# Identity products in TensorE's waits: a two-layer graph and mixer kernel on one core

## The reference, cut to what matters

```python
xn = layernorm(x)                                     # x: 1024 x 512, fp32
x = x + dense_attention(xn, edges) + mixer0(xn)       # one head, 1024 x 1024 mask from edge counts
x = x + quantised_linear(layernorm(x))
xn = layernorm(x)
x = x + gnn(xn, edges) + linear_attention(xn)         # gnn: 2 layers, 8 heads, batch norms, MLP 512-256-512,
                                                      # a layer norm at its end
y = layernorm(x)
x = x + y + nibble_features(y)                        # 6 features a token -> three small MLPs -> 32 columns
```

## Time and profile before

| | |
|---|---|
| Runs, us | 1021.54, 1022.92, 1023.52 (median 1022.92) |
| The profiled execution, us | 1021.41, its span 1019.6 |
| TensorE busy | 951.3 us, 93% of the span |
| VectorE, ScalarE, GpSimd busy | 61%, 48%, 25% |
| Mean granted TensorE clock | 0.986 of 2.4 GHz |
| Chain that ended last | 75% TensorE, 7% GpSimd, 6% VectorE, 3% ScalarE |

### The profile page before, as it was taken

How to read it: one execution, slowest core, us unless ns; L and a number is a source line. 1 busy time by engine, 2 the same in 40 slices (tenths; PEclk the granted TensorE clock), 3 DMA queues, 4 the chain that set the end, 5 groups by cost and what they waited for, 6 DMA issues and landing times.

```text
span 1019.6 us, 15256 instructions
## 1 busy us (share of the span) xinstructions
PE 951.3 (93%) x5371; PEld 678.4 (67%) x5378; DVE 625.5 (61%) x1087; ACT 494.2 (48%) x767; POOL 251.1 (25%) x138
## 2 busy tenths in 40 slices
PE   5999999999998999999999999999999999999915
PEld 2745545788776886886777776746777777777313
DVE  4676466558777325428667776436576666746395
ACT  1655344554724223307666666223476666651054
POOL 2000000499943051310000029112100000570400
PEclk9999999999999999999999999999999999999968
DMA  9201100000200031145655574111065665632102
GB/s 328 76 0 42 42 1 22 1 1 1 83 1 1 3 121 42 58 149 160 190 168 165 176 244 140 42 42 42 14 195 180 187 184 171 226 85 68 38 1 82
DMA packets 58848, 96.14 MB, mean 94 GB/s; under 512 B 8284, under 2 KB 38172, under 8 KB 58270
## 3 DMA queue, kind: packets, MB, share of 16 engines
q1 hardware_dynamic: 55454, 93.11, 28.4%
q10 hardware_dynamic: 3328, 2.15, 0.7%
HBM read 59.58 MB, written 33.55 MB: 91 GB/s over the span
## 4 chain that ended last, share of the span: by engine, by line
PE 75%; POOL 7%; DVE 6%; issue 6%; ACT 3%; DMA 1%; SPq 0%; DVEq 0%; ACTq 0%; POOLq 0%
PE slots L1809 66%; PE slots L1876 9%; POOL MASK L710 3%; POOL MASK L704 1%; POOL KR L709 1%; DMA W<-in_wkT 1%; POOL X L741 1%; POOL PT L701 1%; ACT X L1126 1%; DVE X L1694 0%; POOL WL L721 0%; DVE SM L1671 0%; DVE st L1171 0%; ACT XTR L824 0%; DVE st L1657 0%
## 5 line engine op out<-in xcount | busy, mean ns | idle before, releaser
L1809 PE MATMUL slots<-PT,XN 128*64 128x256 f32 x1024 | 117.6, 382 | 0.2 <-DMA PT<-blocks 0.2
L1809 PE MATMUL slots<-KS,QS 64*128 64x512 f32 x768 | 107.3, 406 | 4.0 <-DVE nm L1599 2.9
L1599 DVE CUSTOM_DVE_ANT_0 SM<-slots,MASK 128x1024 f32<-128x1024 f32 x64 | 75.7, 1220 | 50.6 <-PE slots L1809 50.3
L1809 PEld LDWEIGHTS slots<-PT,XN 128*64 128x64 f32 x1024 | 72.0, 137 | 42.5 <-issue 11.4
L766 POOL TENSOR_TENSOR QS<-QF,QS 128x512 fp32r<-128x512 f32 x16 | 20.7, 1292 | 319.0 <-ACT QS L1046 319.0
L1809 PEld LDWEIGHTS slots<-KS,QS 64*128 64x128 f32 x768 | 72.5, 184 | 22.9 <-issue 9.4
L1030 ACT ACTIVATE SM<-SM,nm 128x1024 f32<-128x1024 f32 x64 | 73.4, 1146 | 24.2 <-DVE nm L1599 23.6
L813 ACT ACTIVATE PT<-slots 128x1024 f32<-128x1024 f32 x68 | 69.3, 1019 | 32.0 <-PE slots L1876 27.1
L1030 ACT ACTIVATE PT<-PT,nm 128x1024 f32<-128x1024 f32 x64 | 73.3, 1145 | 14.7 <-DVE nm L1599 14.0
L1809 PE MATMUL slots<-PT 128*128 128x512 bf16 (+3 forms) x401 | 77.6, 363 | 2.7 <-ACT PT L813 1.2
L1599 DVE CUSTOM_DVE_ANT_0 PT<-slots,MASK 128x1024 f32<-128x1024 f32 x64 | 75.2, 1211 | 4.1 <-PE slots L1809 3.9
(11 more groups left out here) (403 smaller groups left out, 2153.0 us busy)
## 6 DMA issues: line engine op xcount, KB each, us to landing
blocks<-FL SPq DMA_DIRECT2D x56, 512.0 KB, 3.2
PT<-blocks SPq DMA_DIRECT2D x224, 128.0 KB, 3.4
X<-in_x SPq DMA_DIRECT2D x4, 512.0 KB, 11.7
W<-in_wout SPq DMA_DIRECT2D x2, 1024.0 KB, 6.3
W<-in_gq SPq DMA_DIRECT2D x2, 1024.0 KB, 5.0
W<-in_gk SPq DMA_DIRECT2D x2, 1024.0 KB, 5.3
spill<-X SPq DMA_DIRECT2D x4, 512.0 KB, 2.6
SXR<-XTR SPq DMA_DIRECT2D x1, 2048.0 KB, 8.4
```

The lines of the kernel that those rows point to most:

```text
L1599: nc.vector.tensor_tensor_reduce(out=SMs[n % SMB], in0=src, in1=MASK[:, unit(n)[2], :], scale=-1.0, scalar=-0.1 * NO_EDGE, op0=ALU.add, op ...
L1809: return nc.tensor.matmul(o_, lhsT, rhs, start=start, stop=stop)
```

## The change

TensorE multiplies the identity (in one place the identity with the first chunk of XT) into parts of PSUM that a later job overwrites with its own first product: seven times ahead of the waits of "before", six times ahead of the waits for M's weights, twelve times between the turns of chunks 0 to 2 and those of chunk 3, and twice, and nine times with 512 columns, ahead of the wait for the features. Between the last two stands a new wait for six row sums.

```diff
+            def keep_busy(dst, rhs, count):
+
+                for _ in range(count):
+                    mm(dst, ident[:], rhs, True, True)
+
             def mixer_step(name, i):
 
                 slot = begin(name, i)
                 if name == "before":
+                    keep_busy(slot_of("M", 0)[:, 0:P], ident[:], 7)
                     pe.wait_ge(sums_made, 2)
                     pe.wait_ge(bnd_made, 1)
...
                 elif name == "M":
+                    if i == 0:
+                        keep_busy(slot[:, 0:P], ident[:], 6)
                     w_ready(pe, "wqT")
                     w_ready(pe, "wkT")
...
             for j in range(4):
                 begin("gT", j)
                 turn_chunks(j, range(FC - 1))
+            keep_busy(slot_of("gT", 0)[:, (FC - 1) * P:D], ident[:], 12)
             for j in range(4):
                 end(turn_chunks(j, [FC - 1]))
 
+            keep_busy(begin("fT", 0)[:, 0:P], ident[:], 2)
+            wait(y_summed, TT - 2)
+            keep_busy(slot_of("fT", 0)[:, 0:D], XT[:, 0, 0:D], 9)
             pe.wait_ge(hid_ready, 1)
             for q in range(2):
                 slot = begin("fT", q)
```

## The result

| | before | after |
|---|---|---|
| Median of 15 runs, us | 1023.48 (1020.96 to 1025.02) | 1025.91 (1023.45 to 1030.10) |
| Ratio, 95% interval | | 1.0026 [1.0013, 1.0038] |
| The profiled execution, us (its span) | 1021.41 (1019.6) | 1027.32 (1025.5) |
| TensorE busy | 951.3 us, 93% | 969.7 us, 95% |
| Mean granted clock in it, of 2.4 GHz | 0.986 | 0.986 |

The interval is +1.3 to +3.9 us. I had forecast 1023.9 and "within 0.2%" as the likeliest: the time lies in the range given (1022.0 to 1026.0), the change is a small but real loss, and its size, 2.7 us by the ratio, is over two and a half times the 1.0 us that I had forecast (1022.92 to 1023.9). The same kernel before had a median of 1022.92 in its first 3 runs and of 1023.48 in these 15. The page of after has 18 us more of TensorE at work; VectorE (626.0), ScalarE (494.2) and GpSimd (251.2) do the same as before.

What follows compares the result with a forecast made beforehand. TensorE was busy 93%, paced by its sequencer at the start; VectorE and ScalarE set the tail. Terms -0.1 + 0 + 1.6 + 0 + 0.1 = +1.6 on 1021.4 gave 1023.0, plus 0.9 of run excess 1023.9 us; range 1022.0 to 1026.0.

Steps and rivals of the forecast that it cites:

- the credit: Run median's 1.5 us excess over the profiled execution: a late tail clock rise avoided, so only 0.9 us stays.
- M is paced by the sequencer: Start: TensorE's sequencer reading bounds takes 1.98 us a group, so warm multiplications gain only 0.1 us.
- same price: VectorE's register loads cost about 0.5 us each, taken as showing the same price as TensorE's loads in M.
- Seven and six products at 0: Start blocks ahead of "before" and M: they fill waits or their overrun is caught up, cost 0.
- Two MATMULs a product: Twelve products before the last state chunk: 24 instructions, 2.6 us in a 1.0 us hole, cost +1.6 us.
- The rival that a product is one instruction: Block before the last state chunk: products take only 1.3 us, cost +0.3 us, the lower bound; no separate chance given.
- Two products at 0: Two products in fT's slot: four instructions, under 1 us, nothing behind them, cost 0.
- The wide block starts at half rate: Nine wide products before the features: 9.3 to 10.7 us, tail delay 1.6 to 2.4 us, adding 0.1 to the sum.
- rival (a): Slower: clock rises only after 6 us or more of the wide block, all 1.5 us excess stays; 1025.2 us, chance 0.26.
- (b): The runs' whole 1.5 us excess over the profiled execution goes: 1023.0 us or a little less, chance 0.20.
- (c): Faster: M's head start gets through (-0.9), the 1.5 us excess goes, 24 instructions fit their hole; 1020.5 us, chance 0.07.
- (d): Blocks do not act on the clock: wide block runs 15.4 us, 7 us late; 1030 us, chance 0.02.

Runs made afterwards that it cites:

- the repeat: The whole change unchanged, measured again in 12 runs against the kernel before: 1025.83 us against 1023.85, ratio 1.0017 [1.0001, 1.0032].
- all_blocks_spread: The whole change plus the four mixer outputs placed one to a gap, against the kernel before: 1027.37 us, ratio 1.0050.
- no_chunk_block_spread: The change without the twelve products before the last chunk, mixer outputs one to a gap, against the kernel before: 1024.65 us, ratio 1.0021.
- reads_moved_start_blocks: Kernel before with half of the bounds reads moved from M into kq, plus the seven and six start products: 1030.58 us, ratio 1.0074.
- reads_moved: Kernel before with half of the bounds reads moved from M into kq, no identity products: 1028.73 us, ratio 1.0055.
- only_start_blocks: Kernel before with only the seven and six products at the start: 1024.72 us, ratio 1.0002 [0.9987, 1.0017].
- no_chunk_block: The change without the twelve products before the last chunk, old job order, against the kernel before: 1025.51 us, ratio 1.0002.
- fitted_blocks: Kernel before with four products before the last chunk, two small and five wide ahead of the features, none at the start: 1024.22 us, ratio 1.0000.
- gaps_filled: Kernel before with mixer outputs one to a gap, nine products ahead of k1, eight ahead of each layer's gv: 1022.76 us, ratio 0.9990.

## Why the prediction was off: the mechanisms held, the credit did not

- **M is paced by the sequencer: right.** 2.00 us a group against 1.98 predicted; -0.1 predicted, +0.1 measured (17.19 against 17.07), which is no difference either way, and taking half of the reads away made the same warmth worth 2.8 us. The "same price" on VectorE is looser than the text has it: 0.5 us a load there against 1.98 / 3 = 0.66 here.
- **Seven and six products at 0: right.** They end at 8.64 and before 10.9; the wait for wkT still takes 0.98 us. The clock had risen within them (12 instructions in 1.60 us). That a wait is left was luck with wkT: in five of the six other profiles with start blocks M's first product stands right behind the block, yet M takes no longer than in the profiles without them (16.68 to 17.14 us in the four with all reads in place), as the sequencer's beat would have it.
- **Two MATMULs a product, 24 x 0.11 in a hole of 1.0 us, +1.6: right.** 2.68 us between the starts, VectorE 1.61 us later, the tail +1.61 with this block alone. The rival that a product is one instruction is out.
- **Two products at 0: right**, 1.22 us at half rate, nothing behind them.
- **The wide block starts at half rate, ends 9.3 to 10.7 us later, and ScalarE hides most of that: right, with the bound a little short.** 9.46 to 10.86 us in six profiles. By itself +0.14 us; with the chunk block +1.60 to +2.43, against bounds of 1.6 to 2.4 and a middle of 1.7. In three of the six profiles the clock rose late under the block (10.41 us and more), and the wide block's own share of the tail is 0.3 us in the mean of the six, where the sum has 0.1.
- **The Trainium skill's rule, that transposes don't count for the clock** ("TensorE: Matmul & The Clock Gate", Part 4): this case stays with its trace. By that rule the products of hid would begin at half rate in every run of before. In the profile of before they run at full rate behind 16 turns. It is the only one: in the eight other profiles without the features' block hid's first two instructions take 1.06 to 1.18 us instead of 0.70, so there the clock rose only after they had begun.
- **The step that failed is the last of the sum**: "I let a bit over half, 0.9 us, stay", which credits the change with 0.6 of the 1.5 us by which the median stood over the profiled execution, as lost by a late rise in the tail. The late rise exists and is the usual case, but it is cheap: in those eight profiles the 14 products behind it take 3.69 to 4.15 us, 0.16 us over the 3.71 of before in the mean and 0.44 at most. The features' block, which removes it, gained nothing that the runs can tell: 1.0001 [0.9990, 1.0012] alone (this interval by itself would still hold 0.6 us). What the profiled execution lacked lies mostly in the middle. It had about 29 us at half rate: 23.9 in the tail, one dip of 3.4 at 310, and 2 behind TensorE's last work; a mean run has 33 to 36. The middle follows its dips. In the order of jobs of before it is 945.15, 945.19 and 945.72 us in the three profiles with 3.4 us at half rate there, 946.62 with 6.8, and 948.37 to 948.92 in the four with 10.2. Over the runs of before in a set the time goes with the time at half rate (correlation 0.71 to 0.94, 0.26 to 0.36 us each): the 4 to 7 us that the mean run has more make 1.1 to 2.6 us, the size of the excess of 1.5. The dips are a few microseconds each: the one at 310 in all profiles but one, others at 93 to 99, 150, 330, 698 and 973, in other places in each execution.

Redone: without the credit the sum is +1.6 against the median, with 0.3 for the wide block and nothing for the start +1.9. Measured: +1.3 to +3.9, +0.1 to +3.3 in the repeat, +0.2 to +2.9 for the chunk block alone. Of the 2.0 us from 1023.9 to 1025.91, 0.56 is the median of before itself (1022.92 of 3 runs, 1023.48 of 15), 0.6 the credit, 0.3 the wide block and the start; the remaining 0.5 is less than the interval. That 1025.91 still lies in the range is the merit of its upper edge, which was drawn for rival (a), and not of the sum. Rival (a), 1025.2 with the late rise and the whole excess staying, came closest; its late rise under the wide block came in half of the profiles only. Rivals (b) and (c), for which the excess had to go, and (d), a wide block of 15.4 us, did not occur.

**What stays open.** Whether blocks make dips elsewhere more likely. all_blocks_spread at +3.4 to +6.8 us (6 runs) and no_chunk_block_spread at +1.1 to +3.2 us are more than their tails. Both have the start blocks, and so have reads_moved_start_blocks (1.0074 where reads_moved has 1.0055) and a single run of only_start_blocks at 1030.22 us. Against it: only_start_blocks (1.0002) and no_chunk_block (1.0002) as a whole, and a single run of before at 1030.46. The profiles show where some of it lies: in four of the eight with the features' block (all_blocks_spread, no_chunk_block_spread, no_chunk_block, fitted_blocks) the dip at 310 lasts 6.8 us, in none of the nine without it more than 3.4. That block stands 680 us behind the place, so how it could act there is not shown, and one execution each can't decide it.

No kernel beat the one before by more than its interval. The best that the blocks reach is no change, when they are cut to their holes.

## What to carry to other kernels

Size a filler by the instructions that it becomes (a plain fp32 product is two here) and by the hole as the timeline has it: what is over is paid in full when a chain waits behind it. Before warming TensorE, ask who ends last there; a sequencer that reads registers between the products, or the engine that evacuates them, turns a doubled rate into idle time. And don't credit a difference between the profiled execution and the median to one place: look first at the mean clock of every run, since the place may be one that this profile doesn't show.

## What the runs showed of the hardware

- The clock falls while TensorE has no idle time: 100% busy from 145 to 158 and granted 0.50 from 152 on, with products of 34 rows ahead of it (after, and two more profiles with that order). It costs 3.3 us. That the thin products cause it was only argued from the place: the dip at 150 was absent in all six profiles with them spread out, but also in eight of the eleven with them in pairs.
- It also falls after a short rest behind work at full rate: in fitted_blocks it is 1.00 in 1000 to 1005, with 0.39 us of work in the last two, and 0.62 in 1005 to 1008, under unbroken work.
- With its gap of 2.5 us filled the dip at 310 was absent in the one profile of gaps_filled, and another stood at 330. That it moved there is argued from one execution.
- The record of the clock reads 1.00 at the start of an execution while the loads come at 0.85 us, half rate; after 14 and 12 small instructions they come at 0.43.
- A group of three register loads between fp32 products comes every 2.0 us on TensorE's sequencer, as long as 4.6 fp32 MATMULs of 512 columns; two groups ahead of kq leave TensorE idle for 3.8 us.
